# Start of a two-layer kernel: warming products, loads on a second queue, routing before the S4D parameters

## The reference

```python
xn = _layernorm(x)
x = x + _L0_attn_ref(xn, ...) + _L0_ffn_ref(xn, ...)
xn = _layernorm(x)
x = x + _L1_attn_ref(xn, ...) + _L1_ffn_ref(xn, ...)
# layer 0, S4D: the parameters, the kernel K, and a convolution through FFTs
A = -exp(log_A_real) + 1j * A_imag;  dtA = exp(log_dt)[:, None] * A
Ct = (C_re + 1j * C_im) * (exp(dtA) - 1.0) / A
K = 2.0 * real(einsum('hn,hnl->hl', Ct, exp(dtA[:, :, None] * l)))
y = irfft(rfft(x, n=2 * L) * rfft(K, n=2 * L))[:L]
# layer 0, experts: the best two of eight by gate_logits, weighted by a softmax over the two
gate_logits = einsum('bsd,ed->bse', x, Wg)
out = sum over e of gating[e] * (W3[e] @ (silu(W1[e] @ x) * (W2[e] @ x)))
```

## Time and profile before

| | us |
|---|---|
| median of 3 runs | 822.92 (822.19 to 824.34) |
| span of the profiled execution | 820.2 |

### The profile page before, as it was taken

How to read it: one execution, slowest core, us unless ns; L and a number is a source line. 1 busy time by engine, 2 the same in 40 slices (tenths; PEclk the granted TensorE clock), 3 DMA queues, 4 the chain that set the end, 5 groups by cost and what they waited for, 6 DMA issues and landing times.

```text
span 820.2 us, 11626 instructions
## 1 busy us (share of the span) xinstructions
PE 757.8 (92%) x3893; PEld 615.2 (75%) x3893; DVE 658.9 (80%) x1558; ACT 550.4 (67%) x939; POOL 146.5 (18%) x138
## 2 busy tenths in 40 slices
PE   6956366999999998999999999999999999999998
PEld 6624255888888645868788878887888887999997
DVE  7699767899937689998799889976777778877775
ACT  5833123344434368898999899889999997665663
POOL 0067775000000254643044000000000000000000
PEclk9978659899999999999999999999999999999999
DMA  8834582689876512413033112211211210000000
GB/s 251 347 104 137 185 285 90 200 250 289 291 223 195 163 40 70 86 54 89 15 102 81 40 38 59 47 43 44 55 45 49 52 27 0 14 14 20 14 20 27
DMA packets 81274, 85.15 MB, mean 104 GB/s; under 512 B 7361, under 2 KB 59841, under 8 KB 80961
## 3 DMA queue, kind: packets, MB, share of 16 engines
q1 hardware_dynamic: 77120, 76.04, 31.3%
q0 software_dynamic: 4096, 8.40, 3.5%
HBM read 59.12 MB, written 25.30 MB: 103 GB/s over the span
## 4 chain that ended last, share of the span: by engine, by line
PE 75%; POOL 9%; DVE 8%; issue 4%; ACT 3%; DMA 1%; SPq 0%; DVEq 0%; POOLq 0%
PE ps L1829 19%; PE ps L1831 18%; PE ps L1830 18%; POOL x_slots L643 9%; PE ps L1948 6%; PE ps L2024 3%; PE ps L2171 3%; DVE hid_lo L1755 2%; PE ps L1842 1%; PE ps L1927 1%; PE ps L2198 1%; PE ps L1869 1%; PE ps L1848 1%; DVE xn L1436 1%; ACT L880 1%
## 5 line engine op out<-in xcount | busy, mean ns | idle before, releaser
L1755 DVE TENSOR_TENSOR hid_lo<-hid,hid_hi 128x512 fp32r<-128x512 f32 x256 | 175.3, 686 | 52.1 <-ACT hid_hi L881 49.5
L880 ACT ACTIVATE hid<-ps,b_sb 128x512 f32<-128x512 f32 x256 | 177.7, 694 | 36.7 <-PE ps L1831 18.8
L881 ACT ACTIVATE hid_hi<-ps,b_sb 128x512 fp32r<-128x512 f32 x256 | 176.0, 688 | 0.0
L1829 PE MATMUL ps<-hid_hi,w_lo 128*128 128x512 f32 x256 | 102.1, 399 | 5.4 <-DVE hid_lo L1755 5.2
L1829 PE MATMUL ps<-xt_hi,w_lo 128*128 128x512 f32 x256 | 102.4, 400 | 1.5 <-DVE xn L1428 1.5
L1831 PE MATMUL ps<-xt_hi,w_hi 128*128 128x512 f32 x256 | 99.9, 390 | 0.0
L1831 PE MATMUL ps<-hid_hi,w_hi 128*128 128x512 f32 x256 | 99.8, 390 | 0.0
L1830 PE MATMUL ps<-xt_lo,w_hi 128*128 128x512 f32 x256 | 99.8, 390 | 0.0
L1830 PE MATMUL ps<-hid_lo,w_hi 128*128 128x512 f32 x256 | 99.8, 390 | 0.0
L792 ACT ACTIVATE act<-ps 128x512 f32<-128x512 f32 (+1 forms) x57 | 34.0, 596 | 81.6 <-PE ps L1831 81.6
L643 POOL DMA_INDIRECT x_slots<-xn,slot x64 | 71.4, 1115 | 62.6 <-DVE expert_of L1158 43.4
(11 more groups left out here) (337 smaller groups left out, 1543.9 us busy)
## 6 DMA issues: line engine op xcount, KB each, us to landing
gate_row<-gates_dram SPq DMA_DIRECT2D x64, 256.0 KB, 4.8
wc<-w_split SPq DMA_DIRECT2D x57, 256.0 KB, 3.7
w_split<-wc SPq DMA_DIRECT2D x8, 768.0 KB, 4.1
x_slots<-prod SPq DMA_DIRECT2D x11, 512.0 KB, 9.7
xc<-x_slots SPq DMA_DIRECT2D x19, 256.0 KB, 4.3
y_slots<-yo SPq DMA_DIRECT2D x19, 256.0 KB, 4.1
wst<-w SPq DMA_DIRECT2D x16, 256.0 KB, 4.7
wd<-w SPq DMA_DIRECT2D x19, 192.0 KB, 3.1
```

The source lines that it names most:

```text
L880: nc.scalar.activation(hid1[:, u % 4], ps[:, u % 4], ACT.Gelu_apprx_tanh, bias=b1_sb[:, u:u + 1])
L881: nc.scalar.activation(hid1_hi[:, u % 4], ps[:, u % 4], ACT.Gelu_apprx_tanh, bias=b1_sb[:, u:u + 1]).then_inc(hid1_done, 1)
L1755: tt(hid1_lo[:, u % 4], hid1[:, u % 4], hid1_hi[:, u % 4].bitcast(F32), sub).then_inc(hid1_lo_done, 1)
L1829: mm(dst, a_lo, b_hi, start=first, stop=False)
```

## The change

- **PE and DVE:** DVE sets a tile of 128x512 to ones first of all (`warm_done`), and PE multiplies ones by ones four times, 512 columns wide, before the first rows. Their result is not used.
- **Loads:** the small inputs (`wg0`, `log_dt` twice, `state_params`, `wqk_t`, `lag_row`, `prefix`: seven transfers) go from SP's list to the head of ACT's. SP begins with the rows. The zeros of `x_slots` go ahead of the first two expert weights (`w0_load`), and the spare zeros, `wv` and `wg1` behind these. The spare zeros have a semaphore of their own.
- **DVE:** `expm1_start` moves from the head to the place before `scale0(1)`; the series of `expm1_rest` moves to the time between the choice of experts and the ranks; the rest of it, `discretise`, the gates and `discretise_rest` move behind the routing. `scale0(0)` comes after six groups instead of five. The split of `ws` moves behind them.
- **ACT:** all copies of `xt` come earlier, `normalise0` of groups 2 to 7 later, tanh, exp and the sines behind the exponential of the gates.
- **PE:** the product of `wqk` moves behind the ranks; four spectra instead of three lie ahead of the counts; the first K products wait for `ws_lo_done` instead of `slots_done`.
- **POOL:** the scatters wait for `slots_done` 1 instead of 3, for the zeros of `x_slots` without the spare ones, and for each group's normalised rows instead of all.

```diff
@@ -268,6 +268,8 @@
         blanks_out = sem("blanks_out")
+        spare_out = sem("spare_out")
+        warm_done = sem("warm_done")
         member_done = sem("member_done")
...
@@ -462,20 +464,9 @@
         def _(sp):
-            for half in range(2):
-                sp.dma_start(ks[half * N:(half + 1) * N, 0, :],
-                             log_dt[half * HH:(half + 1) * HH].partition_broadcast(N)).then_inc(small_in, 16)
-            sp.dma_start(small[:], state_params).then_inc(small_in, 16)
-            sp.dma_start(wg0_sb[:], wg0).then_inc(wg0_in, 16)
             for g in range(G):
                 sp.dma_start(rows3(g), group(x, g)).then_inc(group_in[g], 16)
-                if g == 1:
-                    sp.dma_start(wqk_sb[:], wqk_t).then_inc(wqk_in, 16)
-            sp.dma_start(consts[:], lag_row.partition_broadcast(P)).then_inc(route_in, 16)
-            sp.dma_start(prefix_sb[:], prefix).then_inc(route_in, 16)
             sp.dma_start(fwd0, dft_fwd).then_inc(fwd0_in, 16)
-            sp.dma_start(wv_sb[:], wv).then_inc(ws_in, 16)
-            sp.dma_start(wsmall[:], wg1).then_inc(ws_in, 16)
...
@@ -483,17 +474,19 @@
-            for e in range(2):
-                w0_load(e)
             sp.wait_ge(blank_done, 1)
...
                              ).then_inc(blanks_out, 16)
+            for e in range(2):
+                w0_load(e)
             spare = y_slots.rearrange("(q p t) h -> p q (t h)", p=P, t=4)[:, SURE_CHUNKS:]
             sp.dma_start(spare, blank.unsqueeze(1).broadcast_to((P, NC - SURE_CHUNKS, W))
-                         ).then_inc(blanks_out, 16)
+                         ).then_inc(spare_out, 16)
+            sp.dma_start(wv_sb[:], wv).then_inc(ws_in, 16)
+            sp.dma_start(wsmall[:], wg1).then_inc(ws_in, 16)
             for e in range(E):
...
@@ -526,7 +519,8 @@
                 down_load(e, q)
-            sp.wait_ge(blanks_out, 16 * (-(-NC // 2) + 1))
+            sp.wait_ge(blanks_out, 16 * -(-NC // 2))
+            sp.wait_ge(spare_out, 16)
             sp.wait_ge(blocks_known, 1)
...
@@ -648,11 +642,12 @@
             rows_of_tile = lambda t: xn[:, t, 0:P]
-            pool.wait_ge(blanks_out, 16 * (-(-NC // 2) + 1))
-            pool.wait_ge(slots_done, 3)
-            pool.wait_ge(xn_ready, G)
+            pool.wait_ge(blanks_out, 16 * -(-NC // 2))
+            pool.wait_ge(slots_done, 1)
             BT = T // BLOCKS
             for t in range(T):
+                if t % B == 0:
+                    pool.wait_ge(xn_ready, t // B + 1)
                 for k in range(2):
...
@@ -705,35 +700,47 @@
-            xt_copy(0)
-            xt_copy(1)
-            act_e.wait_ge(qk_mm, 1)
-            copy(ws_hi[:], ps[:, 4, 0:P]).then_inc(ws_hi_done, 1)
+            act_e.dma_start(wg0_sb[:], wg0).then_inc(wg0_in, 16)
+            for half in range(2):
+                act_e.dma_start(ks[half * N:(half + 1) * N, 0, :],
+                                log_dt[half * HH:(half + 1) * HH].partition_broadcast(N)).then_inc(small_in, 16)
+            act_e.dma_start(small[:], state_params).then_inc(small_in, 16)
+            act_e.dma_start(wqk_sb[:], wqk_t).then_inc(wqk_in, 16)
+            act_e.dma_start(consts[:], lag_row.partition_broadcast(P)).then_inc(route_in, 16)
+            act_e.dma_start(prefix_sb[:], prefix).then_inc(route_in, 16)
+            for g in range(4):
+                xt_copy(g)
             root0(0)
-            for g in range(2, 4):
-                xt_copy(g)
-            for g in range(4):
+            xt_copy(4)
+            normalise0(0)
+            xt_copy(5)
+            normalise0(1)
+            xt_copy(6)
+            xt_copy(7)
+            root0(1)
+            for g in range(2, 5):
                 normalise0(g)
-                xt_copy(g + 4)
-            root0(1)
+            spectrum_copy(0)
+            normalise0(5)
+            act_e.wait_ge(counted, 1)
+            copy(counts[:], ps[:, 6, 0:2 * P].rearrange("p (a t) -> p a t", a=2)).then_inc(counts_copied, 1)
+            for g in range(6, G):
+                normalise0(g)
+            for n in range(1, 4):
+                spectrum_copy(n)
+            act_e.wait_ge(top2_done, 1)
+            nc.scalar.activation(p2, m2, ACT.Exp).then_inc(top2_exp_done, 1)
             act_e.wait_ge(decay_done, 1)
...
             nc.scalar.activation(ks[:, 8], ks[:, 12], ACT.Sin, scale=TWO_PI / 2).then_inc(trig_done, 1)
-            for g in range(4, 6):
-                normalise0(g)
-            for n in range(2):
+            for n in range(4, 6):
                 spectrum_copy(n)
-            act_e.wait_ge(counted, 1)
-            copy(counts[:], ps[:, 6, 0:2 * P].rearrange("p (a t) -> p a t", a=2)).then_inc(counts_copied, 1)
-            for g in range(6, G):
-                normalise0(g)
-            act_e.wait_ge(top2_done, 1)
-            nc.scalar.activation(p2, m2, ACT.Exp).then_inc(top2_exp_done, 1)
-            for n in range(2, 6):
-                spectrum_copy(n)
+            act_e.wait_ge(qk_mm, 1)
+            copy(ws_hi[:], ps[:, 4, 0:P]).then_inc(ws_hi_done, 1)
             act_e.wait_ge(ws_in, 32)
...
@@ -763,7 +770,8 @@
                 spectrum_copy(n)
-            act_e.wait_ge(blanks_out, 16 * (-(-NC // 2) + 1))
+            act_e.wait_ge(blanks_out, 16 * -(-NC // 2))
+            act_e.wait_ge(spare_out, 16)
             for c in range(KC):
...
@@ -935,6 +943,7 @@
             a_im, c_re, c_im = small[:, 1], small[:, 2], small[:, 3]
+            nc.vector.memset(xt[:, 1], 1.0).then_inc(warm_done, 1)
             step.mark(nc.vector.memset(eps[:], LN_EPS))
...
@@ -989,12 +998,16 @@
-            def expm1_rest():
+            def expm1_series():
...
                     v = step.mark(stt(PP, PP, 1.0 / math.factorial(k), R, add, mul))
+            def expm1_rest():
+                need(step.n)
                 power = exp2[:].rearrange("p (a h) -> p a h", a=2)
...
@@ -1070,16 +1083,13 @@
                 v = step.mark(ts(K(21), K(19), -1.0, None, mul))
-            expm1_start()
-            for g in range(5):
+            for g in range(6):
                 moments0(g, signal=(g == 3))
             scale0(0)
-            for g in range(5, G):
+            for g in range(6, G):
                 moments0(g, signal=(g == G - 1))
-            expm1_rest()
+            expm1_start()
             scale0(1)
-            dve.wait_ge(ws_hi_done, 1)
-            tt(ws_lo[:], ps[:, 4, 0:P], ws_hi[:].bitcast(F32), sub).then_inc(ws_lo_done, 1)
...
@@ -1087,7 +1097,7 @@
             v = step.mark(tt(eq, means, wsum, mul))
-            need(v)
+            need(step.n)
             dve.wait_ge(route_in, 32)
...
@@ -1110,14 +1120,7 @@
             tt(m2, m2, m1, sub).then_inc(top2_done, 1)
-            discretise()
-            dve.wait_ge(top2_exp_done, 1)
-            v = step.mark(ts(p1, p2, 1.0, None, add))
-            need(v)
-            v = step.mark(nc.vector.reciprocal(p1, p1))
-            need(v)
-            step.mark(tt(gate2[:], p2, p1, mul))
-            step.mark(nc.vector.tensor_copy(xn[:, :, P], p1))
+            expm1_series()
...
@@ -1165,6 +1168,18 @@
+            expm1_rest()
+            discretise()
+            dve.wait_ge(top2_exp_done, 1)
+            v = step.mark(ts(p1, p2, 1.0, None, add))
+            need(v)
+            v = step.mark(nc.vector.reciprocal(p1, p1))
+            need(v)
+            step.mark(tt(gate2[:], p2, p1, mul))
+            step.mark(nc.vector.tensor_copy(xn[:, :, P], p1))
+            discretise_rest()
+            dve.wait_ge(ws_hi_done, 1)
+            tt(ws_lo[:], ps[:, 4, 0:P], ws_hi[:].bitcast(F32), sub).then_inc(ws_lo_done, 1)
             dve.wait_ge(ws_hi_done, 2)
...
@@ -1173,7 +1188,6 @@
-            discretise_rest()
             FH, FL, AR, CTR, CTI = K(15), K(16), K(4), K(19), K(22)
@@ -1831,6 +1845,9 @@
+            pe.wait_ge(warm_done, 1)
+            for _ in range(4):
+                mm(ps[:, 3], xt[:, 1, 0:P], xt[:, 1], start=True, stop=True)
             pe.wait_ge(ident_done, 1)
...
@@ -1847,9 +1864,6 @@
                 last.then_inc(xt_done, 1)
-                if g == 1:
-                    pe.wait_ge(wqk_in, 16)
-                    mm(ps[:, 4, 0:P], wqk_sb[:, 0], wqk_sb[:, 1], start=True, stop=True).then_inc(qk_mm, 1)
                 if g >= 1:
...
@@ -1870,10 +1884,10 @@
+            pe.wait_ge(wqk_in, 16)
             pe.wait_ge(fwd0_in, 16)
-            spectra(range(3))
+            spectra(range(4))
             pe.wait_ge(member_done, 1)
-            pe.wait_ge(ws_lo_done, 1)
             pe.wait_ge(ident_done, 2)
...
@@ -1883,10 +1897,11 @@
             mm(ps[:, 7, 0:T * E], before[:], chosen, start=False, stop=True).then_inc(ranked, 1)
-            spectra(range(3, 16))
+            mm(ps[:, 4, 0:P], wqk_sb[:, 0], wqk_sb[:, 1], start=True, stop=True).then_inc(qk_mm, 1)
+            spectra(range(4, 16))
             for c in range(KC):
                 pe.wait_ge(tables_done, c // 2 + 1)
```

(2 more changed lines are left out.)

## The result

| | before | after |
|---|---|---|
| median of 6 runs | 823.36 us (822.19 to 824.34) | 827.37 us (824.89 to 829.69) |
| ratio | | 1.0050 (95% interval 1.0035 to 1.0065) |
| span of the profiled execution | 820.2 | 827.9 |

The change costs about 4 us, where 823.3 was forecast with a range up to 826.5. The two profiled executions lie at opposite ends of their kernels' ranges (time less span is 1.8 us), so their spans differ by 7.7, and not all of that is the change's. A second profile of the same kernel stands among the experiments for that reason.

A forecast was written before the change was run, and what follows sets the result against it. The start of `angles` was taken as the bound: routing 6.1 us earlier, 6.5 us queued behind it, so `angles` 0.4 us later and 823.3 us. Likeliest case's range 821.4 to 825.8; 8-in-10 range 820.4 to 826.5.

The forecast's parts named there:

- The bound: Start of chunk 1's full PE stretch: set by the parameter chain from `angles` at 49.12, scatters having 1.7 us to spare.
- The change as a trade: DVE up to `angles`: routing gains 6.1 us, 6.5 us queued behind it give that back; `angles` at 49.5 against 49.12.
- The second term: DVE work between slots and `angles`: 11.6 us instead of 5.14.
- the first term: End of routing: slots stand at 37.9 instead of 43.98, 6.1 us earlier, bounds 36.0 and 44.5.
- Products of ones: PE's start: level rises after 3.6 us of dense work, first transposes at 7.0, 0.6 us lost.
- The loop: PE's loop over groups: high level for about four groups, then ACT sets the pace; logits end at 22.0, 5.4 us earlier.
- The spectra: Four spectra on PE ahead of the counts: start 22.7 to 23.0, 3.6 us at low level, done at 31.7.
- Members, ranks, slots: Routing: choice of experts takes 6.37 us, counting and ranking 2.66, slots 3.34.
- The price of one microsecond: Conversion of a shift in `angles` into run time, taken one for one; `angles` 0.4 us later.
- The loop stays slow: Rival: PE's level falls when the products end, logits at 26.8, `angles` at 54.2, time 828; chance 0.16.
- The scatters set the end: Rival: the end follows the first scatter, 7.1 us earlier, giving 816; chance 0.05.
- The gap before chunk 1: Rival: earlier rows keep PE's level high around its pause there, winning 2.9 us, 820.4; chance 0.12.

The follow-up runs named there:

- late angles: Kernel before with six settings of an unused tile on DVE right ahead of `angles`: 827.68 us, ratio 1.0051.
- filled gap: Kernel after with `expm1_rest` and `discretise` moved from behind the slots into DVE's wait for the ranks: 820.55 us, ratio 0.9971.
- late scatters: Kernel before with three, then twelve settings of an unused tile on POOL ahead of the scatters: 823.40 and 822.97 us.
- one spectrum ahead: Kernel after with one spectrum instead of four ahead of the counting of members on PE: 824.02 us, ratio 1.0014.
- three settings ahead of its scatters: Kernel before with three settings of an unused tile on POOL ahead of the scatters: 823.40 us, ratio 0.9996.
- release edit: Kernel before with only the scatters' release changed: first slots signal, chunks' zeros without the spare ones, each group's rows; 823.56 us, ratio 0.9999.
- no products: Kernel after without the four products of ones and their memset: 825.92 us, ratio 1.0036.
- filled pauses: Unused PE products, two and three, behind the first and second turn of inputs: kernel after 823.87 us; with series in DVE's gaps and one spectrum ahead 818.01.

## Why the prediction was wrong

*The bound* was right: the scatters don't set the end, and what counts is when `angles` starts. The late angles, the filled gap and the late scatters each show it.

*The change as a trade* was right in form: 6.1 us gained by the slots, 6.5 more queued behind them. The second term measured 11.71 against 11.6 forecast from slots to `angles`. **The step that failed is the first term:** slots at 37.9 were forecast, 40.72 and 39.19 measured, so 3.3 to 4.8 us earlier and not 6.1. (The prediction's own summands, 34.4 and 3.34, give 37.7.) What failed in it is the size of the path through ScalarE's list and the four spectra; its parts:

- *Products of ones:* first transposes at 7.86, forecast 7.0; the level rose at 6.92, 5.4 us into the products and not 3.6. "0.6 us is lost here" was worse than that sounds: I measured the price against the old arrival of the rows at 6.40, but with the rows issued first PE could start at 4.22. The price is 3.6 us.
- *The loop:* from the first transposes to the end of the logits it took 15.98 us, forecast 15.0; with the later start that is 23.84 instead of 22.0. Four groups at the high level were taken and about four came (four transposes take 0.63 us instead of 1.09), but their four copies were done 4.78 us after the first transposes and not 3.7. From there on ScalarE's list sets the pace, as forecast, and took 11.2 us against 11.3. How long the level stays high hardly matters then: with one spectrum ahead it held to 16.7, and the loop took the same 15.98.
- *The spectra:* they waited for the rows that ScalarE normalises, started at 24.68 instead of 23.0 and ran at the low level for 6.1 us (2.8 in the second profile); the forecast took 3.6 from one execution of before. They end at 34.66 and 33.13, forecast 31.7. The first lies beyond the bound of 33.4, because that bound had no later start in it: I added up ends for each step and not the worst of two steps in a row.
- *Members, ranks, slots:* 2.67 and 3.35, as in the earlier trace rows.

So `angles` starts 1.8 to 3.3 us later, not 0.4.

*The price of one microsecond.* I took one for one. A delay of 3.43 us cost 4.5 (2.9 to 5.5), the kernel after's 1.8 to 3.3 cost 3.0 to 4.0, and what the filled gap won in `angles` brought more than itself too. The first is within its interval of one for one. For the rest the profiles show where it can come from: both of the kernel after, and that of the late angles, have a second low stretch within chunk 0's products, and there it is 23.0 to 23.1 us from the turn of chunk 0's rows to that of chunk 2's, against 21.1 in the kernel before and with the gap filled. But the profile of the kernel before with three settings ahead of its scatters has it too, 23.1 us with `angles` at 48.65, taken in the longest of its executions (825.45), and its median is that of before; a shorter one (21.9 us) stands in those of the release edit, of one spectrum ahead and of no products. So the second stretch comes without any late `angles`. Whether a late `angles` makes it more frequent, and so explains the extra 1 us, is open. In the twelve executions of the second run of the kernel after the level and the time go together: the three with the highest mean granted clock (0.958) took 824.3 to 824.8 us, the six with the lowest (0.949 to 0.952) 826.4 to 829.1.

*The rivals.* "The loop stays slow" had 828 and a chance of 0.16. The time came near that, but not by its mechanism: the level fell only at the fourth group, logits ended at 23.84 and not 26.8, and `angles` stood at 52.43 and not 54.2. That its number is near is chance. "The scatters set the end" is refuted. "The gap before chunk 1": the change didn't win the level there, and 2.9 us was too high a price for that one stretch (filled pauses brought 0.8 in the median where it alone could be won, with intervals that overlap); the 3 us of the kernel after are for two.

*The range.* The upper end of the likeliest case's range, 825.8, stood on the transfers issued by ACT (2.5 us), which cost nothing: ACT's list was ready at 6.05, ahead of the first copy. The prediction's own bound for the slots, 44.5, stood beside it and went into no sum. The terms that rest on PE's level, products, loop and spectra, all uncertain to the same side, should have set the range.

## What to carry to other kernels

Before work is moved behind a chain on one engine, look for the idle time of that engine ahead of the chain's next wait: here 4.8 us stood empty in front of the ranks while 5.1 us of the same engine's work were queued behind the slots, and moving them there turned a loss of 4 us into a gain of 2.6. Price a warm-up against the time at which the engine could start without it, not against the time at which it started before. And where several terms hang on the same uncertain thing (here TensorE's level), add their bad ends together.

## What the runs showed of the hardware

- TensorE's level fell at 13.74 while the engine was busy 6.59 of the last 6.84 us, in a loop of 128x128 transposes and 8-column products (in three other kernels with the same loop it held to between 16.7 and 17.0), and came back in the dense spectra only after 2.8 us in one execution and 6.1 in another of the same kernel.
- Four transposes of 128x128 took 1.09 us at the low level and 0.63 at the high one; the product of `prefix` 2.13 and 1.16.
- The 64 scatters took between 83.8 and 89.6 us from the first start to the last in the profiles of the kernel before and of three made from it; what sets their pace isn't shown.
- Seven transfer issues on ScalarE's queue took from 0.80 to 4.74 us, 0.56 each, against 0.61 for SP's first pair.
